# A graph network on one core: the adjacency turned chunk by chunk into banks of its own, the first aggregation in three groups of products, and the opening products of zeros run twice

## The reference, cut to what matters

```python
# x: (16, 512, 128), adj: (512, 512), about 2 nonzeros a row plus the diagonal
def L0(x, adj, weight, bias):
    y = einsum('nm,bmf->bnf', adj, x) + x
    y = einsum('bnf,fo->bno', y, weight) + bias
    return y / max(sqrt(sum(y * y, axis=2)), 1e-12)
def L1(h):                                   # 5 times, in and out matrix are both adj
    m = einsum('nm,bmd->bnd', adj, h); av = concat(m, m)
    z = sigmoid(av @ w3.T + b3 + h @ u3.T + ub3); r = sigmoid(av @ w4.T + b4 + h @ u3.T + ub3)
    hv = tanh(av @ w5.T + b5 + (r * h) @ u5.T + ub5)
    h = (1 - z) * h + z * hv
# L2: normalised (adj + I), then a weight; L3: softmax over values of e where adj > 0
x = layernorm(x + L0(x)); x = layernorm(x + L1(x)); x = layernorm(x + L2(x)); x = layernorm(x + L3(x))
```

## Time and profile before

| | |
|---|---|
| Median of three runs | 771.02 us (769.65 to 773.0) |
| Profiled execution, its own time | 769.01 us |
| Span in the trace | 767.1 us |
| PE busy, share of the span | 751.2 us, 98% |
| DVE, ACT, POOL busy | 624.6, 513.7, 166.2 us |
| Mean granted clock of PE | 0.998 |

### The profile page before, as it was taken

One profiled execution on the slowest core, in us unless ns is written; L12 is line 12 of the kernel. 1 busy time (PEld: TensorE's weight loads), 2 busy tenths in 40 slices (PEclk: granted clock), 3 DMA queues, 4 the chain that ended last, 5 costly groups with the idle time before them and its releaser, 6 DMA issues.

```text
span 767.1 us, 11992 instructions
## 1 busy us (share of the span) xinstructions
PE 751.2 (98%) x3788; PEld 630.1 (82%) x3788; DVE 624.6 (81%) x1447; ACT 513.7 (67%) x1072; POOL 166.2 (22%) x314
## 2 busy tenths in 40 slices
PE   8999999999999999999999999999999999899996
PEld 7888788888888888888888888888887887789885
DVE  5899998888888788877777777887999998785663
ACT  4799877666667766666666666666587857875444
POOL 1778420000000000000000000000123257764334
PEclk9999999999999999999999999999999999999999
DMA  7500000000030001000000000000000000000112
GB/s 226 204 1 2 1 1 1 1 1 1 0 117 1 1 1 56 1 0 1 1 1 0 0 0 0 0 0 2 1 1 1 1 1 1 3 14 28 56 56 83
DMA packets 9895, 16.60 MB, mean 22 GB/s; under 512 B 2929, under 2 KB 4465, under 8 KB 9201
## 3 DMA queue, kind: packets, MB, share of 16 engines
q1 hardware_dynamic: 9840, 15.94, 6.1%
HBM read 8.59 MB, written 5.24 MB: 18 GB/s over the span
## 4 chain that ended last, share of the span: by engine, by line
PE 78%; DVE 9%; ACT 7%; POOL 2%; issue 2%; DMA 1%; SPq 0%; DVEq 0%; ACTq 0%
PE agg_ps L971 12%; PE agg_ps L973 12%; PE agg_ps L972 12%; PE gate_ps L907 7%; PE gate_ps L909 6%; PE gate_ps L908 6%; PE cand_ps L907 4%; PE cand_ps L909 4%; PE cand_ps L908 4%; PE turn_ps L1010 4%; PE gate_ps L914 2%; PE cand_ps L914 2%; DVE stats L810 2%; ACT res L428 2%; ACT feat L505 1%
## 5 line engine op out<-in xcount | busy, mean ns | idle before, releaser
L971 PE MATMUL agg_ps<-adj_hi,nat_hi 128*128 128x512 f32 x384 | 152.1, 396 | 0.0
L973 PE MATMUL agg_ps<-adj_hi,nat_lo 128*128 128x512 f32 x384 | 150.1, 391 | 0.0
L972 PE MATMUL agg_ps<-adj_lo,nat_hi 128*128 128x512 f32 x384 | 149.6, 390 | 0.0
L629 POOL TENSOR_SCALAR shift<-mean_var 128x4 f32<-128x4 f32 x64 | 25.6, 400 | 427.1 <-DVE mean_var L814 424.8
L767 DVE TENSOR_TENSOR agg_lo<-agg_ps,agg_hi 128x512 fp32r<-128x512 f32 x80 | 55.2, 690 | 65.0 <-ACT agg_hi L457 65.0
L490 ACT ACTIVATE reset_hi<-gate_r 128x512 fp32r<-128x512 f32 x80 | 50.6, 633 | 83.1 <-DVE gate_r L784 83.1
L973 PEld LDWEIGHTS agg_ps<-adj_hi,nat_lo 128*128 128x128 f32 x384 | 72.1, 188 | 16.2
L972 PEld LDWEIGHTS agg_ps<-adj_lo,nat_hi 128*128 128x128 f32 x384 | 72.2, 188 | 15.6
L971 PEld LDWEIGHTS agg_ps<-adj_hi,nat_hi 128*128 128x128 f32 x384 | 72.1, 188 | 15.4 <-DVE adj_lo L833 0.3
L474 ACT ACTIVATE gate_r<-gate_ps,bias 128x512 f32<-128x512 f32 x80 | 55.2, 690 | 43.5 <-PE gate_ps L909 43.5
L457 ACT ACTIVATE agg_hi<-agg_ps 128x512 fp32r<-128x512 f32 x80 | 48.7, 608 | 45.3 <-PE agg_ps L973 45.3
(11 more groups left out here) (181 smaller groups left out, 1794.2 us busy)
## 6 DMA issues: line engine op xcount, KB each, us to landing
res<-in_x SPq DMA_DIRECT2D x16, 256.0 KB, 5.3
out<-res SPq DMA_DIRECT2D x16, 256.0 KB, 2.0
rows<-in_adj SPq DMA_DIRECT2D x4, 256.0 KB, 4.0
adj_hi<-eye_hi SPq DMA_DIRECT2D x1, 1024.0 KB, 9.6
adj_lo<-eye_lo SPq DMA_DIRECT2D x1, 1024.0 KB, 11.5
later<-in_adj SPq DMA_DIRECT2D x1, 1024.0 KB, 6.5
mix_rows<-mix SPq DMA_DIRECT2D x1, 1024.0 KB, 8.0
later<-mix_rows SPq DMA_DIRECT2D x1, 1024.0 KB, 4.9
```

The costliest lines, as they stand in the source:

```text
L971: pe.matmul(ps, nat_hi[:, b, k, :], m_hi[:, k, :], start=(k == 0), stop=False)
L972: pe.matmul(ps, nat_hi[:, b, k, :], m_lo[:, k, :], start=False, stop=False)
L973: last = pe.matmul(ps, nat_lo[:, b, k, :], m_hi[:, k, :], start=False, stop=(k == T - 1))
```

## The change

The transposes of chunk t now go to bank t, columns k, so that a bank is complete with its chunk and `eye_turned` counts after each one. ACT copies bank t to the columns t of all four blocks of `eye_hi`; its copy of graph 0 moves from ahead of the four to ahead of the last. DVE's four remainders follow the same way and stand between the masks, `x_lo(0)` ahead of the last. The first aggregation issues four products high x high, then four with `nat_lo`, then four with `eye_lo`, and waits ahead of each group; it needs all of `eye_hi` at its start. The products of zeros are issued a second time, and ACT's first seeding waits for all eight. Units from 1 on are as before.

```diff
@@ ACT, opening
-            act.wait_ge(x_in[0], 16)
-            act.activation(nat_hi[:, 0, :, :], res[:, 0, :, :], ACT.Copy).then_inc(x_hi_made, 1)
-            for k in range(T):
-                act.wait_ge(eye_turned, k + 1)
-                act.activation(eye_hi[:, k, :], prep_ps[k][:, :], ACT.Copy).then_inc(eye_hi_made, 1)
+            for t in range(T):
+                if t == T - 1:
+                    act.wait_ge(x_in[0], 16)
+                    act.activation(nat_hi[:, 0, :, :], res[:, 0, :, :], ACT.Copy).then_inc(x_hi_made, 1)
+                act.wait_ge(eye_turned, t + 1)
+                act.activation(eye_hi[:, :, t * P:(t + 1) * P], prep_ps[t][:, :].rearrange("p (k i) -> p k i", k=T),
+                               ACT.Copy).then_inc(eye_hi_made, 1)
@@ ACT, slot 0
-                        act.wait_ge(bits_set, len(layer_ps))
+                        act.wait_ge(bits_set, 2 * len(layer_ps))
@@ DVE, opening (behind mask of chunk t)
-            x_lo(0)
-
-            for k in range(T):
-                dve.wait_ge(eye_hi_made, k + 1)
-                dve.tensor_tensor(eye_lo[:, k, :], prep_ps[k][:, :], eye_hi[:, k, :].bitcast(F32),
-                                  ALU.subtract).then_inc(eye_lo_made, 1)
-            x_lo(1)
-            x_lo(2)
+                if t == T - 1:
+                    x_lo(0)
+                dve.wait_ge(eye_hi_made, t + 1)
+                cols = slice(t * P, (t + 1) * P)
+                dve.tensor_tensor(eye_lo[:, :, cols], prep_ps[t][:, :].rearrange("p (k i) -> p k i", k=T),
+                                  eye_hi[:, :, cols].bitcast(F32), ALU.subtract).then_inc(eye_lo_made, 1)
+            for b in range(1, 3):
+                x_lo(b)
@@ PE, opening
-            for ps in layer_ps:
+            for ps in layer_ps + layer_ps:
...
-                    block = prep_ps[k][:, t * P:(t + 1) * P]
+                    block = prep_ps[t][:, k * P:(k + 1) * P]
...
-                    if t == T - 1:
-                        last.then_inc(eye_turned, 1)
+                last.then_inc(eye_turned, 1)
@@ PE, slot
-                        pe.wait_ge(x_lo_made, s + 1)
+                        if s:
+                            pe.wait_ge(x_lo_made, s + 1)
...
+                    if s == 0:
+                        pe.wait_ge(eye_lo_made, 1)
+                        pe.wait_ge(eye_hi_made, T)
+                        pe.wait_ge(x_hi_made, 1)
+                        for k in range(T):
+                            pe.matmul(ps, nat_hi[:, b, k, :], m_hi[:, k, :], start=(k == 0), stop=False)
+                        pe.wait_ge(x_lo_made, 1)
+                        for k in range(T):
+                            pe.matmul(ps, nat_lo[:, b, k, :], m_hi[:, k, :], start=False, stop=False)
+                        pe.wait_ge(eye_lo_made, T)
+                        for k in range(T):
+                            last = pe.matmul(ps, nat_hi[:, b, k, :], m_lo[:, k, :], start=False, stop=(k == T - 1))
+                    else:
+                        # the loop over k of before, without its wait for eye_lo_made
```

More of the change, by code:

```diff
@@ L965, in slot @@
                     b, ps = s % B, agg_ps[s % 2][:, :]
[L966 to L973, removed]
+                    if s == 0:
[11 more added lines that the diff above has]
+                    else:
+                        for k in range(T):
+                            if s == AFTER + B:
+                                pe.wait_ge(turn_read, reads(TURN_NO["mix", k]))
+                            pe.matmul(ps, nat_hi[:, b, k, :], m_hi[:, k, :], start=(k == 0), stop=False)
+                            pe.matmul(ps, nat_hi[:, b, k, :], m_lo[:, k, :], start=False, stop=False)
+                            last = pe.matmul(ps, nat_lo[:, b, k, :], m_hi[:, k, :], start=False, stop=(k == T - 1))
                     last.then_inc(agg_done, 1)
```

## The result

| | before | changed |
|---|---|---|
| Median of 22 runs | 769.3 us (768.67 to 773.0) | 768.43 us (767.93 to 769.46) |
| Ratio, 95% interval | | 0.9985 [0.9979, 0.9991] |
| Profiled execution, own time | 769.01 us | 767.93 us |
| Span in the trace | 767.1 us | 766.1 us |

The change is worth 0.9 us by the medians and 0.7 to 1.6 by the interval: within 0.5%, as forecast, and clear of no change, which the interval excludes. The forecast time, 770.5, and the lower end of its range, 768.6, were too high. The measured kernel lies at 768.43.

A forecast was written before the change was run, and what follows sets the result against it. The prediction took PE, busy 751.2 of 767.1 us, as the bound. Starting the second aggregation at 12.37 instead of 12.89 gained 0.52 us, so 771.02 - 0.5 = 770.5 us, range 768.6 to 772.5.

The forecast's parts named there:

- The sum: Whole kernel: a gain of 0.5 us, giving 768.5 for an execution like the profiled one and 770.5 from the median 771.02.
- Step 1: PE's opening: four more products of zeros put the first transpose at 4.68, 0.59 us after chunk 0 has landed.
- Step 2: PE's clock in the opening: rises to 2.4 GHz at 6.0 instead of 9.0, after 4.9 us of unbroken work.
- Steps 3 and 4: PE's transposes and ACT's copies in the opening: transposes end at 8.2 (now 9.29), PE has its high parts at 9.2.
- Step 4: ACT in the opening: three bank copies hidden in idle time, bank 3's copied 8.52 to 9.12; alone a 0.9 us gain.
- Step 5: DVE in the opening: becomes the last, `nat_lo` starts at 9.79, and PE waits 0.36 us for it inside the first aggregation.
- Step 7: Behind the first aggregation: later work moves with it, landings have at least 0.5 us of slack, so the 0.52 stays.
- The low clock: Rival, PE's opening: transposes stay at 0.213 us each, second aggregation at 13.56, 0.67 us later than now, 771.7; chance 0.15.
- given back: Rival, first layer: something there is timed by more than the first aggregation, so the gain is 0, 771.0; chance 0.15.
- The whole gain: Rival, opening: the clock rises before 5 us, second aggregation at 12.0, 0.9 us gained, 770.1; chance 0.15.
- Its own sign of being wrong: Opening: the prediction is wrong if the second aggregation, forecast at 12.37, starts after 12.9.

The follow-up runs named there:

- e3: The changed kernel with the first aggregation block by block again, waiting for the last of the four remainders at its start: 770.25 us, ratio to before 1.0006.
- e4: The changed kernel with DVE's masks of chunks 1 to 3 moved behind `nat_lo` of graph 1: 768.7 us, ratio to before 0.9980.
- e1: The changed kernel with the products of zeros run once, as before: 769.05 us, ratio to before 0.9985.
- e2: The kernel before with the products of zeros run twice and nothing else: 769.47 us, ratio to before 0.9995.
- e6: The kernel before with POOL's addition of the layernorm epsilon left out: 765.57 us, ratio to before 0.9962.

## Why the prediction was wrong, point by point

- *The sum.* The step that failed is the last of the sum, "the median of the runs shown is 2.0 above that one, so the forecast is 771.02 - 0.5 = 770.5". The median of three, with one of 773.0, was 1.7 above what 22 runs gave (769.3). The other number of the same paragraph, 768.5 for an execution like the profiled one, would have been right. The range was built around 771.02 as well, and its lower end missed by 0.2; with 769.3 in its place the forecast is 768.8. The term of the gain was too small too: 0.5 against a measured 0.9.
- *Step 1* held: 4.69 against 4.68.
- *Step 2*, the clock. Right in kind, 0.9 us late (6.9 against 6.0). In the other traces of the changed kernel the rise came at 4.7 and 5.4, and in those of before at 9.0, 10.5 and 9.1. So the distance of 4.9 us from one trace was no rule: the rise differs between executions.
- *Steps 3 and 4.* PE's start was 9.70 and not 9.2. Step 4 put `nat_hi` at 7.98, "bound by its landing", and took that landing as fixed; `x` landed at 8.4, 8.9 and 8.4 in the three traces of the changed kernel and at 8.0, 8.3 and 8.3 in those of before. Chunk 2 ended at 8.0 instead of 7.28, but its copy was done at 8.50, so three copies were hidden but for 0.1. (In e3's trace, where `x` landed at 7.9, that copy did hold `nat_hi` up, to 8.56.) A copy in four pieces cost 0.5 a step, as a plain one.
- *Step 5.* DVE's row came out as forecast (`nat_lo` at 9.81, forecast 9.79), but as PE was late itself, there was no wait inside the first aggregation (2.83 us from its first product to the second aggregation, against 2.81 before), though 0.36 was forecast. None of the other traces of this opening has one either. Two errors of opposite sign, 0.5 lost by the landing and 0.36 not lost to DVE, left the gain at 0.36 in this trace, where 0.52 was forecast: that the size is near is luck.
- *Step 7*, "so the 0.52 stays". What the opening gave was passed on whole, as e3 shows in the other direction. But the step looked only for landings that could take something back, and not for waits that another meeting of POOL and DVE would change. That wait, 1.2 to 1.9 us, holds the other half of the difference between the kernels' traces. Whether the change favours the short one is open: the changed kernel had 1.2 in three traces of three, the three of before 1.9, 1.5 and 1.6, but e4's program had both, e1 had 1.9 and e2, with the opening of before, 1.2. So how the measured 0.9 divides between opening and wait stays open: with equal landings the opening alone would give 0.9.
- *The rivals.* The low clock did not stay. By the rule of the Trainium skill, TensorE: Matmul & The Clock Gate, in its part on PE-mode transpose, full rate does not engage in transposes, which would have meant that; here the rise at 6.9 fell amid them and they went on at 0.12. Nothing was given back. The whole gain of 0.9 was there in every trace of the changed opening when it is counted from the start of `nat_hi`, with a late rise of the clock (6.9) as with an early one (4.7); as the two profiled traces stand beside each other it was 0.36.
- *Its own sign of being wrong*, a second aggregation after 12.9, came in one trace of the changed kernel (12.93) with the mechanism intact. The sign should have been counted from the landing.
- *What no part named*: an early rise in the kernel before lengthens PE's pause, and the clock may fall again, as in e2's trace. A third of the executions of before on one chip took 1.8 us more, for which this is the likely cause. The changed kernel has none above 769.5 in 34, but beside those runs before had few over 770.5 too (2 of 22 and 1 of 21). On the chip of the third, e1 and e4, with the changed kernel's banks, have none in 22.

## What to carry to other kernels

Anchor a forecast on the profiled execution when the median stands on three runs that spread by 3 us, and let the range reach down to it. Where a stretch begins with a landing, count its milestones from that landing: here that turned second aggregations anywhere from 12.3 to 13.0 into one number, 4.0. Preparing a matrix piece by piece, with the consumer's products ordered by which operand is ready first, is worth what it takes off the first product's start and no more; the order of the products is what makes it pay (e3). Look for the place where a slow helper engine's small instructions set the longest wait: here one instruction of 0.24 us per layernorm was worth 3.3 us, nearly four times the 0.9 of the change.

## What the runs showed of the hardware

- PE's clock rose at 6.9 us behind unbroken work from 1.11, and at 9.0 behind work from 4.09; other traces of the same two kernels have 4.7 and 5.4, 10.5 and 9.1. It fell back in two traces. In e2, behind a pause of 1.73 us, the granted clock was 0.54 from 11.0 to 14.7. In e4, behind a wait of 1.9 us, it was 0.50 from 647.6 to 651.0. Pauses of 1.4 (e6), 1.9 (before) and 2.6 us (e3) passed without a fall.
- The same load of 256 KB, issued at 2.65 us behind the same others, took 5.2 to 6.3 us to land.
- The stages' column of the granted clock says 1.00 in the first microseconds, where records 0.21 and 0.43 apart show the 1.2 GHz level.
- A POOL addition on 128 x 4 took 0.23 us alone and 0.55 or 0.82 beside DVE's, and which of two that start 0.04 to 0.05 us apart wins differed between traces.
